# A mixer and expert block on one core: four loads in another order, centring in two halves, four taps scaled by ScalarE, and a new order of steps

## What is computed

```python
x = x + conv_block(layernorm_over_channels(x))      # the mixer
t = tokens(x)                                       # (16, 256, 64)
t = t + experts(layernorm(t))                       # 8 experts, top 2 of a softmax
```

```python
zxbcdt = einsum('bhwc,oc->bhwo', x, W_in)           # z 128, x 128, B and C 32, dt 8
dt = softplus(zxbcdt[..., 288:] + dt_bias)
xBC = silu(depthwise_conv_3x3(xBC, conv_w) + conv_b)
KV = einsum('bln,blhd->bhnd', Bm, xs * (dt * exp(A_log)))
y = einsum('bln,bhnd->blhd', Cm, KV) + xs * D
y = layernorm(y * silu(z)) * ln_g + ln_b
out = einsum('bld,od->blo', y, W_out)
```

## Time and profile before

| | us |
|---|---|
| median of 3 runs | 160.89 (160.42 to 161.43) |
| the profiled execution | 161.06 |
| its span, first to last instruction | 158.8 |
| PE busy in the span | 143.4 |

### The profile page before, as it was taken

One profiled execution on the slowest core, in us unless ns is written; L12 is line 12 of the kernel. 1 busy time (PEld: TensorE's weight loads), 2 busy tenths in 40 slices (PEclk: granted clock), 3 DMA queues, 4 the chain that ended last, 5 costly groups with the idle time before them and its releaser, 6 DMA issues.

```text
span 158.8 us, 3263 instructions
## 1 busy us (share of the span) xinstructions
PE 143.4 (90%) x1106; PEld 57.3 (36%) x1106; DVE 112.3 (71%) x294; ACT 93.8 (59%) x178; POOL 80.4 (51%) x149
## 2 busy tenths in 40 slices
...
GB/s 106 193 16 12 172 30 0 4 4 2 0 0 4 0 8 206 244 83 2 0 0 34 246 233 32 66 0 46 252 231 15 66 12 191 228 111 0 0 66 70
DMA packets 9658, 11.87 MB, mean 75 GB/s; under 512 B 4130, under 2 KB 7594, under 8 KB 9642
## 3 DMA queue, kind: packets, MB, share of 16 engines
...
...
## 4 chain that ended last, share of the span: by engine, by line
PE 64%; DVE 21%; issue 5%; ACT 3%; DMA 3%; SPq 1%; DVEq 0%; ACTq 0%
PE pm L1060 14%; PE pe L1165 8%; PE pe L1180 8%; PE pe L1060 5%; PE pm L1180 5%; PE pm L1165 5%; DVE tmp L939 4%; DMA cw_x<-in_L_conv_conv_w_dram 3%; PE pr L1124 2%; PE pm L1070 2%; PE pr L1110 2%; DVE x L903 2%; PE pm L1078 2%; DVE g L874 1%; DVE xo L898 1%
## 5 line engine op out<-in xcount | busy, mean ns | idle before, releaser
L472 POOL TENSOR_TENSOR acc<-acc,tmp 128x256 f32<-128x256 f32 x54 | 38.3, 733 | 21.7 <-DVE tmp L939 20.9
L636 ACT ACTIVATE hid<-pe,b1T 128x512 f32<-128x512 f32 x48 | 30.2, 681 | 10.5 <-PE pe L1165 10.4
L1165 PE MATMUL pe<-fst,w 64*128 64x512 f32 x96 | 26.5, 627 | 1.4 <-ACT hid L636 1.4
L1180 PE MATMUL pe<-hid,w 128*32 128x512 f32 x192 | 25.5, 601 | 0.9 <-DVE tmp L939 0.6
L939 DVE SCALAR_TENSOR_TENSOR tmp<-pe,b2T,gates 128x512 f32<-128x512 f32 x24 | 17.9, 745 | 10.6 <-PE pe L1180 10.6
L1060 PE MATMUL pm<-pad,wT 64*128 64x512 f32 x108 | 25.1, 600 | 0.0
L663 DVE SCALAR_TENSOR_TENSOR bcc<-bcp,cw_bc,bcc 128x256 f32<-128x256 f32 x32 | 15.5, 483 | 0.9
L636 ACT ACTIVATE hid<-pm,b1T 128x512 f32<-128x512 f32 x16 | 10.1, 684 | 8.7 <-PE pm L1165 6.3
L1060 PEld LDWEIGHTS pm<-pad,wT 64*128 64x128 f32 x108 | 9.9, 185 | 11.9 <-issue 11.9
L417 POOL TENSOR_TENSOR r<-ve,halves 128x8 f32<-128x8 f32 x3 | 5.0, 1676 | 17.7 <-DVE ve L784 17.7
L1165 PEld LDWEIGHTS pe<-fst,w 64*128 64x128 f32 x96 | 7.8, 185 | 15.1 <-issue 15.0
...
## 6 DMA issues: line engine op xcount, KB each, us to landing
gates<-cwd SPq DMA_DIRECT2D x32, 256.0 KB, 5.7
xin<-in_x_dram SPq DMA_DIRECT2D x6, 128.0 KB, 3.4
out_dram<-acc SPq DMA_DIRECT2D x6, 128.0 KB, 2.5
w<-in_L_ffn_W_dram SPq DMA_DIRECT2D x2, 256.0 KB, 4.9
xin<-in_x_dram ACTq DMA_DIRECT2D x2, 128.0 KB, 4.2
w<-in_L_ffn_W_dram ACTq DMA_DIRECT2D x1, 256.0 KB, 4.4
...
out_dram<-acc SPq DMA_DIRECT2D x2, 64.0 KB, 2.3
```

The source lines that it names most:

```text
L472: ins = pool.tensor_tensor(acc[p][:, half], (x2 if e == 0 else acc)[p][:, half], tmp[ln][e % 2][:, half], ALU.add)
L636: act.activation(hid[ln][e % 2][:, q, :], expert_banks(g)[q][:], ACT.Gelu, bias=b1T[:, e:e + 1]).then_inc(hid_in[ln].sem, 1)
L1165: ins = pe.matmul(expert_banks(g)[q][:], w1[half, place(e, q), :], fst[p][half, :], start=True, stop=True)
L1180: ins = pe.matmul(bank[C * q + c:C * q + c + BC, half], w2[:, e, c:c + BC], hid[ln][e % 2][:, q, half], start=True, stop=True)
```

## The change

1. SP's loads: `cw_x` is issued second and has a count of its own; then B, C and dt's part (`wbd_raw`), the z part, also on a count of its own, both halves of `xin1` (the second was ACT's), and then the first half of `w1`.
2. The step `twc` is split in `twx` and `twz`: the x part and the z part are centred each by itself, in 128 columns. `tTb` waits for both.
3. `tpa`, the first four taps, is now done by ACT in four instructions with a scale from each partition's `cw_x`. `tpb` stays on DVE.
4. The count `i_w1` is split in two, one for each copy of the centred `w1`. `bd0` waits only for that which frees its bank.
5. `PLAN` is another: the order of the steps differs from the head to about `u22`, two thirds of its length, and in single places after it.

```diff
-busy0 busy0 busy0 busy0 busy0 busy0 sq0 sx0 twc0 sm0 busy0 busy0 busy0 ve0 busy0 busy0 tb0 wa0 sr0 tpa0 tw0 rw0
...
+busy0 busy0 busy0 busy0 busy0 busy0 busy0 sq0 sx0 twx0 sm0 tpa0 busy0 tb0 busy0 busy0 twz0 tTa0 tpb0 tw0 sq1
...
             load(0, (0,))
-            sp.dma_start(wxz_raw[:, 1], twice(W_in[0:DI, :])).then_inc(d_proj, 16)
-            sp.dma_start(cw_x[:], cw_v[0:DI, :]).then_inc(d_proj, 16)
+            sp.dma_start(cw_x[:], cw_v[0:DI, :]).then_inc(d_cwx, 16)
+            sp.dma_start(wbd_raw[:], twice(W_in[2 * DI:2 * DI + BC + NH, :])).then_inc(d_wbd, 16)
+            sp.dma_start(wxz_raw[:, 1], twice(W_in[0:DI, :])).then_inc(d_z, 16)
+            load(1)
             sp.dma_start(w1[0:C, :, :], W1.rearrange("e c f -> c e f")).then_inc(d_w1, 16)
-            sp.dma_start(wbd_raw[:], twice(W_in[2 * DI:2 * DI + BC + NH, :])).then_inc(d_wbd, 16)
-            load(1, (0,))
...
+                elif step == "tpa":
+
+                    act.wait_ge(i_tap, 2)
+                    act.wait_ge(d_cwx, 16)
+                    for t in range(4):
+                        act.activation(taps[:, t, :], wxz[:, 0].rearrange("p r c -> p (r c)"), ACT.Copy,
+                                       scale=cw_x[:, t:t + 1]).then_inc(i_tpa, 1)
...
-                    if g == 0:
-                        act.dma_start(xin[1][C:2 * C, :].rearrange("c (b l) -> c b l", b=2), x_v[1, 1]).then_inc(d_x[1], 16)
...
-                elif step == "twc":
-                    dve.wait_ge(d_proj, 16 * 3)
...
+                elif step in ("twx", "twz"):
+
+                    n = int(step == "twz")
+                    c = (i_tap, i_twz)[n]
+                    dve.wait_ge((d_proj, d_z)[n], 16)
+                    dve.reduce_sum(wxz_sum[:, 2 * n:2 * n + 2], wxz_raw[:, n], axis=AX.X).then_inc(c, 1)
+                    dve.wait_ge(c, 1)
+                    dve.scalar_tensor_tensor(out=wxz[:, n], in0=wxz_sum[:, 2 * n:2 * n + 2].unsqueeze(2)
+                                             .broadcast_to([P, 2, C]), scalar=-1.0 / C, in1=wxz_raw[:, n],
+                                             op0=ALU.mult, op1=ALU.add).then_inc(c, 1)
...
-                    pe.wait_ge(i_tap, 3 if step == "tTa" else 4)
+                    if step == "tTa":
+                        pe.wait_ge(i_tpa, 4)
+                    else:
+                        pe.wait_ge(i_tap, 3)
+                        pe.wait_ge(i_twz, 2)
...
-                        pe.wait_ge(i_w1, 2)
+                        pe.wait_ge(i_w1[1], 1)
```

More of the change, by code:

```diff
@@ L18 @@
 PLAN = """
-busy0 busy0 busy0 busy0 busy0 busy0 sq0 sx0 twc0 sm0 busy0 busy0 busy0 ve0 busy0 busy0 tb0 wa0 sr0 tpa0 tw0 rw0
[L20 to L32, removed]
-pw23 d71 h02 a61 m71 rx23 u12 rt03 rb23 a71 h12 d02 xn23 th3 u22 st1 m02 rt13 u03 a02 h22 d12 h03 rt23 u32 m12
@@ L34 @@
-cwt3 d03 cwc3 h32 gw3 a12 d22 u13 m22 u42 a22 h13 d32 h42 u23 m32 u52 a32 h23 d42 h52 u33 m03 u62 m42 a03 d13
-d52 m13 h33 a42 d23 m52 h62 a13 u43 m23 d62 h43 a23 d33 m62 a52 u53 m33 u72 h53 a62 d43 h72 a33 u63 m43 d72 h63
-a43 d53 m72 u73 a72 m53 d63 h73 a53 st2 m63 d73 a63 m73 a73 st3
+busy0 busy0 busy0 busy0 busy0 busy0 busy0 sq0 sx0 twx0 sm0 tpa0 busy0 tb0 busy0 busy0 twz0 tTa0 tpb0 tw0 sq1
+busy0 ve0 tTb0 ta0 ini0 sr0 wa0 tea0 rw0 tec0 rb0 wbe0 sm1 xn0 teb0 dt0 cv00 dt10 ve1 ea0 dtv0 pw1 ex0 wae0 sf00
@@ new lines @@
+bd0 cv10 bcp0 sf10 rx1 k00 k10 cv20 nm0 sf20 k20 rb1 xs00 z0 xs10 xn1 bcs0 dt11 xt00 sz00 nT0 v00 sz10 xt10 ne0
+bt0 v10 bd1 btc0 sq2 dtv1 kv0 bcp1 c00 sq3 kvc0 k01 sm2 y0 ve2 cv01 ex1 y00 pw2 sf01 cv11 rx2 gs00 y10 sf11 cf0
+k11 gs10 rb2 ps0 xn2 pj0 gst0 bd2 sf21 pwg0 cv21 bcp2 k21 pc0 rxg0 dt12 k02 rbg0 cv02 x20 xs01 bcs1 xs11 k12
+sq20 z1 dtv2 xt01 k22 sz01 s20 sz11 xt11 ve20 bt1 cv12 v01 pw20 ex2 btc1 v11 sf02 rx20 kv1 rt00 sf12 rb20 cv22
+kvc1 th0 rt10 y1 xn20 xs02 rt20 bcs2 z2 xs12 sz02 y01 cwt0 xt02 cwc0 sz12 xt12 gw0 y11 u00 bt2 h00 sf22 pj1 v02
```

41 lines of the change are left out of this document (25 added, 16 removed).

## The result

The changed kernel takes 159.8 us (median of 11 runs, 159.4 to 160.73) against 160.82 of the kernel before beside it (11 runs, 160.06 to 161.43): a ratio of 0.9946, 95% interval 0.9929 to 0.9962. That is 0.5% faster: the interval excludes no change, but the difference is smaller than the 1% that the prediction takes as the least that counts as one. It is 0.2 from the 159.6 forecast, and inside its range of 158.3 to 161.6. The profiled execution took 159.5, its span is 157.3 where it was 158.8.

What follows compares the result with a forecast made beforehand. The prediction took TensorE's work, its standing still, and the head and tail as the bound. Its terms, -0.25 - 0.3 - 1.1 - 0.3 + 0.7 = -1.25, gave a median of 159.6 us, range 158.3 to 161.6.

Steps and rivals of the forecast that it cites:

- Term A: Head: the second convolution piece starts at 15.55 instead of 15.80, -0.25 us, between -1.2 and +0.9.
- the part that I called free: Head: four tap scalings on ScalarE, 1.1 us at most, cost nothing because ScalarE was idle there.
- Term B: Near 26 us: moving `nT0` and `c00` removes the wait for `wo`, -0.3 us, between -0.65 and +0.2.
- Term C: Near 60 us: `kvc2` first and `u10` ahead remove PE's wait for `kv`, -1.1 us, between -1.15 and 0.
- Rival 3: From about 60 us VectorE carries the end, so Term C and Term D are given back: 161.0 us, chance 0.12.
- Term D: Near 93 us: moving `s22` back removes PE's wait for its squares, -0.3 us, between -0.3 and 0.
- Term E: Head to about `u22`, places unknown: new waits from moved steps in in-order queues, +0.7 us, between 0 and +2.0.
- Rival 1: Whole kernel: everything comes and nothing is lost, -2.4 us, 158.5 us, chance 0.22.
- Rival 2: Head: loads come late, `w1` landing at 9.9 or later; 160.5 us, chance 0.12.
- Rival 4: Near 65 us: `m00` ahead of `y02` waits for the gates' load, +1.8 us, 162.7 us, chance 0.10.
- the 9.0 to 9.9 that I named as a sign: Head: `w1` landing between 9.0 and 9.9 us in the profile after would support the forecast.

Runs made afterwards that it cites:

- taps_on_vector: The changed kernel with its first four taps scaled by VectorE again, in one product: 159.29 us (4 runs), ratio 0.9907 to the kernel before.
- sums_back: The changed kernel with group 1's sums `sm1` behind the first convolution piece again: 164.06 us (4 runs).
- kv_back: The changed kernel with `kv2` behind `ps1` and `kvc2` behind `gst1` again, `u10` still ahead: 161.09 us, ratio 1.0035 to the kernel before.
- head_rows: taps_on_vector with VectorE's and TensorE's head steps reordered and `nT0` ahead of `z0`: 159.85 us, ratio 0.9932 to the kernel before.
- the first half alone: The changed kernel with the new order only up to `rb1`, the old order behind: 160.16 us, ratio 0.996 to the kernel before.
- oldhead_newrest: The kernel before with its own code and order up to `rb1`, the new order behind: 160.02 us, ratio 0.9955 to the kernel before.

## Why the prediction was right, point by point

- **The total** was right, 159.6 against 159.8, and the sum of -1.25 against a measured -0.94 at `d73` and -1.0 in the medians. Its terms were not all right, and that it came so near is in part luck: by the starts, A was 0.35 better than forecast, B 0.23 and E some 0.5 worse. C, the term with a test of its own, carries the result.
- **Term A**, forecast -0.25, was -0.60 (`cv10` 15.73 to 15.13). Mis-sized by two steps. I had `wa0` set by `w1` landing at 9.05 to 9.9; `w1` was issued at 4.64, near the forecast 4.8, but `wa0` started at 9.16 behind `tTb0`, and this stood behind VectorE's row and the z half's load. The way by `ve0` and `r1w`, which I had at 10.0, was ready at 10.20. So `rb0` was at 10.25, not 10.4. And I kept the 1.82 between `rb0` and `cv00` (1.75 by the starts of the timeline), though those rows of before held `dt0` and `tTb0` on PE, and `tTb0` moved out; it was 1.53. The third part, 0.43 for `sm1`, was right: with `sm1` back, `rb0` to `cv10` takes 0.44 longer. `cw_x` at 5.35 and z at 6.9 bracket my 5.9 and 6.6. Of the part that I called free, the scalings on ScalarE, the duration was over my upper bound (1.28 for 1.1) and it cost nothing; but taps_on_vector shows no gain by it either.
- What I left out of A: that `sm1` has to be early once `ve1` is early on VectorE. sums_back shows 2.0 us lost without it, and 4.3 with the clock; in the changed kernel nothing of this was at stake.
- The size of A also hangs on when loads land: in traces with these loads in this order, `rb0` started at 10.13 to 10.44.
- **Term B**, forecast -0.3, was about -0.07 at `ps0`. The wait for `wo` went, and 0.16 for `v` and 0.26 for group 0's `kv` took its place. `c00` covered only part of the time until `kvc0`, where I had it cover all. That `kv0` would come up to 0.4 later was in my text: its lead is 0.31 where that at `cv10` is 0.60.
- **Term C**, forecast -1.1, was right. kv_back loses 1.15 at `d73` and 1.3 in the median. Rival 3, that VectorE gives it back, falls with it.
- **Term D**, forecast -0.3, agrees with the trace: the wait of 0.3 ahead of `s22` is gone. The 0.9 that PE still waits for squares is at `s21` (0.36, new) and `s23` (0.49, where it was 0.87). No run has this move alone.
- **Term E**, forecast +0.7, a sum without places. Now they have names, by PE's idle stretches in the timeline of the changed kernel: 0.26 ahead of `u10`, 0.15 ahead of `u40` and 0.36 ahead of `s21` (the lock, on `x`), 0.51 ahead of `ps3`, 0.50 ahead of `u03`, and `cwt2` with 0.83 where it and `d31` had 0.27 and 0.39: 1.95 in all. Others went that I had not counted: 0.83 ahead of `cwt3`, 0.46 ahead of `u11`, 0.38 of the 0.87 ahead of `s23`. All idle stretches of PE from 12 us on sum to 7.8 before and 6.9 after. Less B, C and D, that leaves +0.6. By the starts it is more: -0.94 less -0.60, -0.07, -1.15 and -0.3 for A to D leaves +1.2. The two ways differ by 0.6, since ends of matmuls are modelled; the forecast lies between them. The starts show where most of it was lost: from `u11` to `u51` the lead falls from 1.36 to 0.30.
- **Rival 1**, all comes and nothing is lost: A (even -0.60 for its -0.55) and C came in full, but E did too. **Rival 2**, late loads: not in the changed kernel, but head_rows shows that with its engines a little earlier the loads do bind, at 9.09. **Rival 4**: no wait for gates; `m00` ran at 62.72, the gates issued from 57.07.
- When `w1` lands: 4.1 after its issue in the changed kernel, by 8.7, and not 5.1 after; that is earlier than the 9.0 to 9.9 that I named as a sign. The Trainium skill ("DMA: Bandwidth & Descriptors", section "Queues, rings and completion order") says that each DMA engine takes descriptors in ring order and goes round between the queues. The trace is in line with this: the 9.05 that I worked out from the bytes is nearer to it than the 9.9 by `w1`'s own row. It was no bound there, so the 0.3 it would have added never counted.

The two halves don't add up: 0.93 and 0.47 apart, 0.94 together. Of the missing 0.46, 0.34 is the idle piece of VectorE at 71.2 in the trace of before, which the first half alone had won; the new order has the lock's 0.5 in either case (in oldhead_newrest the product takes 1.28 too, with both engines starting at 65.60 and 65.61, and so does `x`). What decides from run to run whether VectorE or GpSimd is first is open.
